# Causal attention of a two-layer kernel: scores from stacked split products, keys masked on GpSimd, values projected behind the experts

## Chip, cores and metric

One core of one Trainium2 chip. The metric is the device time of one execution in microseconds; the engines are TensorE (PE, its weight loads PEld), VectorE (DVE), ScalarE (ACT), GpSimd (POOL) and SyncE (SP, which here issues DMAs).

## The reference, cut to what matters

Two layers run on 16 sequences of 100 rows of 256 values. Each layer is a cross attention over a context and a mixture of experts, each on normed rows and added to them. The change touches the second layer's attention and its neighbours:

```python
qp = q @ Wq.T                                   # q: layernorm of x, 16 x 100 x 256
kv = latent_kv @ Wkv_expand.T                   # latents 64 wide -> keys and values of 256
...                                             # 16 heads of 16 columns
scores = einsum('bhqd,bhkd->bhqk', qh, kh) * HD ** -0.5
scores = where(tril(ones((100, 100))), scores, finfo.min)
out = einsum('bhqk,bhkd->bhqd', softmax(scores), vh)
...
return out @ Wout.T
```

Only the first 100 context rows of a sequence take part, since the mask is causal. Ahead of it stands the first layer's mixture of experts: 8 experts, two per row, hidden width 688.

## The kernel before

**Order of the stages.** After the first layer's attention comes the dispatch of the rows to experts (`Dispatch`, lines 1050 to 1391), in one block of `gated_moe`. Scores choose two experts for each row; products on TensorE (`tensor_lists`, line 1228) list which row goes to which place; DVE turns that into indices (lines 1378 to 1380), and POOL gathers the first 128 rows by an indirect DMA (line 1459). TensorE and ScalarE also make the keys (`project_keys`, 2106, moved by 2122) and values (`project_values`, 2115, moved by 2128) of the second layer's attention in that block, nine sequences' values ahead of the list products and seven behind. Each block ends with a barrier of all engines.

Then `gated_experts` takes up to 32 tiles of 128 rows. ScalarE and DVE split an expert's weights into a high and a low fp32r part (1682, 1729), TensorE multiplies three split products (`split_products`, 183), turns and multiplies down. ScalarE may begin a tile's weights when SP has announced that expert's load (`announce`, 1438); in the block SP issues two tiles' down weights (1444) and the loads of experts 5 to 7 (1433) first. The results come back by DMA and DVE adds them to X (1768).

**Norm and query projection.** `causal_attention` calls `layernorm`: on DVE a chain of small dependent instructions on 100x16 values (124 to 139, with a square root on ScalarE), the normed rows (143), transposes on TensorE, and the split into XH (ScalarE, 160) and XL (DVE, 149). In the next block DVE splits the query weights (2179, 2180), TensorE makes eight 128x400 pieces of the queries, six fp32r products each, and ScalarE and DVE copy four each to QT (2173, 2186).

**The attention loop.** 18 steps, pipelined over sequences i; each sequence has two halves u of 8 heads (n = 2i + u), and each half two groups g of 4 heads with a PSUM bank each.
- DVE `operands`: `kb` is the half's keys repeated for 8 heads, times 0 or 1 so that each head keeps its own 16 rows (2343, 128x800), and `qb` a copy of the queries (2345).
- PE `scores`: per group one fp32 product of 128 rows by 400 columns (2246) and one bf16 product that adds the causal mask (2248).
- DVE `maxima`: two reductions (2353) and a multiplication by -SCALE (2357).
- ACT `exps`: eight exponentials of 100x100 with their sums (2313).
- PE `turn`: eight transposes (2259); ACT and DVE `move` one bank each (2319, 2361); PE `values`: eight products of 16 columns (2272).
- DVE scales O (2389, 2394); PE turns it (2285), ACT copies it (2331), PE multiplies by Wout (2296), DVE adds X (2383).

The order on each engine is written out by hand in `step`. On PE it is scores(i, 0), transposes of O of i-2, turn and values of older halves, scores(i, 1), turn(2i), Wout, values.

Of the kernel before, what the change touches and what calls it, by code (L numbers as in the profile page):

```python
# [82 lines left out]

def layernorm(core, tag, X, XN, ident, XH, XL, known=0, loads=None, first=None, arrive=None, ident_in=None):

# [5 lines left out]
    with ExitStack() as ctx:  # L91
# [1371 lines left out]
def gated_moe(core, dram, X, ident, normed, results, causal):  # L1463

    nc = core.nc
    KEYS_FIRST, VALUES_FIRST = 5, 9
    with ExitStack() as ctx:
        weights = GatedWeights(core, ctx, dram)
        rows = GatedRows(core, ctx)
        with ExitStack() as stage:  # L1470
            d = Dispatch(core, ctx, stage, dram, "m0_", X, ident, E0, TOK0, False, normed,
                         (weights.rows, None, weights.places))
            latents = CausalLatents(core, stage, dram)
            with nc.Block() as block:

                @block.sync
                def _(sp):
# [8 lines left out]
                    weights.load_down(sp, d.tile_expert, 0)  # L1486
                    sp.wait_ge(d.rows_stored, 16)
# [9 lines left out]
                def _(pe):  # L1497
# [4 lines left out]
                    causal.project_values(pe, latents, range(VALUES_FIRST))  # L1502
                    d.tensor_lists(pe)
                    causal.project_values(pe, latents, range(VALUES_FIRST, B))

                @block.scalar
                def _(act):
# [4 lines left out]
                    causal.move_values(act)  # L1512
# [5 lines left out]
        gated_experts(core, X, ident, d, weights, rows, results, causal)  # L1518


def gated_experts(core, X, ident, d, weights, rows, results, causal):
# [9 lines left out]
    with ExitStack() as ctx:  # L1531
# [42 lines left out]
        with nc.Block() as block:  # L1574

            @block.sync
            def _(sp):
# [4 lines left out]
                for e in range(E0):  # L1582
                    weights.announce(sp, e)
# [28 lines left out]
            def _(pe):  # L1612
# [53 lines left out]
                down(k, 1)  # L1666

            @block.scalar
            def _(act):
# [48 lines left out]
                hidden_out(tiles - 1, 1)  # L1718

# [411 lines left out]

def causal_attention(core, dram, X, ident, causal, later):

    nc, psum = core.nc, core.psum
    HT = H // KD
    SCALE = HD ** -0.5
    wq, wo, mask, blocks, KTT, V = causal.wq, causal.wo, causal.mask, causal.blocks, causal.KTT, causal.V
    with ExitStack() as ctx:
        XH = fixed(ctx, nc, "XH_c", [P, KD, B * S], F32R)
        XL = fixed(ctx, nc, "XL_c", [P, KD, B * S], F32R)  # L2140
        wqh = fixed(ctx, nc, "c_wqh", [P, KD, D], F32R)
        wql = fixed(ctx, nc, "c_wql", [P, KD, D], F32R)
        maskb = fixed(ctx, nc, "c_maskb", [S, S], BF16)
        identb = fixed(ctx, nc, "c_identb", [S, S], BF16)
        QT = fixed(ctx, nc, "c_QT", [P, KD, B * S])

        with ExitStack() as stage:
            XN = fixed(stage, nc, "XN_c", [S, B, D])
            layernorm(core, "ln2_", X, XN, ident, XH, XL, B - 1, later)

        parts = core.sem("ca_parts")
        chain = core.sem("ca_chain")
        proj = core.sem("ca_proj")

        tiles = [(k, c) for c in range(NC) for k in range(KD)]

        with nc.Block() as block:

            @block.tensor
            def _(pe):  # L2160
                pe.wait_ge(parts, 1)
                for n, (k, c) in enumerate(tiles):
                    cols = slice(c * CH, (c + 1) * CH)
                    last = split_products(nc, psum[n][:, 0:CH], [(wqh[:, j, k * P:(k + 1) * P], wql[:, j, k * P:(k + 1) * P],
                                                                  XH[:, j, cols], XL[:, j, cols]) for j in range(KD)])
                    last.then_inc(proj, 1)

            @block.scalar
            def _(act):
                for n in range(0, len(tiles), 2):  # L2170
                    k, c = tiles[n]
                    act.wait_ge(proj, n + 1)
                    nc.scalar.activation(QT[:, k, c * CH:(c + 1) * CH], psum[n][:, 0:CH], ACT.Copy)

            @block.vector
            def _(v):
# [58 lines left out]
        with nc.Block() as block:  # L2235

            @block.tensor
            def _(pe):
# [99 lines left out]
            def _(v):  # L2338
# [28 lines left out]
                def step(i, w):  # L2367
                    n = i * 2
                    if has(i, 0, B - 1):
                        maxima(i, 0)  # L2370
# [193 lines left out]
```

## Time and profile before

| | us |
|---|---|
| median of 3 runs | 1821.97 (1820.47 to 1822.61) |
| profiled execution | 1817.92 |
| its span | 1816.1 |

| engine | busy share of the span |
|---|---|
| PE | 89% |
| PEld | 61% |
| DVE | 68% |
| ACT | 41% |
| POOL | 51% |

The span runs from the first to the last instruction of the profiled execution; the execution's own time is 1.8 us longer. Shares are averages over stages with different limits, so the rows below are read stage by stage: stretches of the span first, then groups of instructions of one stage, then single instructions in order of time. Times in the rows count from the span's start. A group's line gives its total and mean duration, and behind the second bar the idle time of its engine just before it with what ended that idle time.

### The profile page before, as it was taken

How to read it: one execution, taken by the hardware profiler on the slowest of the kernel's cores; microseconds unless marked ns; L12 is line 12 of the kernel's file. 1: busy time of each engine (PE TensorE's matmuls, PEld its weight loads, DVE VectorE, ACT ScalarE, POOL GpSimd, SP SyncE). 2: the span in 40 equal slices, each digit the busy share in tenths (PEclk: the TensorE clock that was granted, in tenths of full speed). 3: DMA queues.
4: the chain of work that ended last, by engine and by line, in shares of the span. 5: the costliest groups of instructions: out<-in, count | busy, mean ns of one | idle time of the engine just before them, and what ended most of it. 6: DMA issues, size and time to landing. Idle time of an engine off the chain costs nothing. (4 is left out here: it accounts for less than half of the span.)

```text
span 1816.1 us, 27644 instructions
## 1 busy us (share of the span) xinstructions
PE 1622.1 (89%) x8770; PEld 1110.5 (61%) x8770; DVE 1230.1 (68%) x2197; ACT 742.8 (41%) x1965; POOL 921.1 (51%) x799
## 2 busy tenths in 40 slices
PE   5999977999999999999999996799999289978980
PEld 4667744555555555555555553499999167665870
DVE  5598768777787777777787744466666757756433
ACT  3100102444444444444444452466666156652220
POOL 0377747777888777777888452023332000000636
PEclk9999987999999999999999997699999699988895
DMA  6434344122212221222212002664444420001443
GB/s 199 134 67 96 69 106 136 42 79 79 79 41 75 79 70 52 79 78 79 79 39 77 10 11 87 211 196 130 132 139 116 156 58 1 0 4 37 123 112 108
DMA packets 91472, 157.41 MB, mean 87 GB/s; under 512 B 45841, under 2 KB 70645, under 8 KB 88077
## 3 DMA queue, kind: packets, MB, share of 16 engines
q1 hardware_dynamic: 84301, 138.86, 26.2%
q0 software_dynamic: 7040, 16.92, 3.2%
q8 instruction: 67, 1.10, 0.3%
q14 instruction: 64, 0.52, 0.1%
HBM read 125.31 MB, written 28.48 MB: 85 GB/s over the span
## 5 line engine op out<-in xcount | busy, mean ns | idle before, releaser
L897 ACT ACTIVATE R<-banks 128x400 f32<-128x400 f32 x768 | 326.7, 509 | 317.9 <-PE banks L931 317.1
L713 DVE TENSOR_REDUCE PM<-banks 128x2 f32<-128x964 f32 x320 | 360.9, 1133 | 137.7 <-PE banks L690 137.6
L751 POOL TENSOR_TENSOR EA<-EA,R 128x400 f32<-128x400 f32 x288 | 306.1, 1063 | 119.2 <-ACT R L897 105.8
L931 PE MATMUL banks<-QS,KH 128*128 128x400 f32 x768 | 288.8, 376 | 2.3 <-DMA QB<-ML 2.3
L931 PE MATMUL banks<-QB,KB 128*128 128x400 f32 x768 | 265.7, 346 | 0.0
L731 DVE TENSOR_TENSOR banks<-banks,R 128x400 f32<-128x400 f32 x320 | 183.8, 574 | 27.9 <-ACT R L897 26.7
L540 POOL TENSOR_TENSOR arena<-arena 96x400 f32<-96x400 f32 x128 | 141.4, 1125 | 115.8 <-DVE arena L515 115.6
L941 PE MATMUL banks<-R,KV 128*64 128x400 f32 x960 | 187.5, 512 | 0.0
L931 PEld LDWEIGHTS banks<-QS,KH 128*128 128x128 f32 x768 | 145.1, 189 | 54.5 <-issue 38.0
L690 PE MATMUL banks<-KH,QS 64*128 64x482 f32 x320 | 160.6, 503 | 17.2 <-DVE PM L713 7.7
L690 PEld LDWEIGHTS banks<-KH,QS 64*128 64x128 f32 x320 | 60.7, 190 | 160.7 <-DVE PM L713 86.4
L690 PE MATMUL banks<-KH,QB 64*128 64x482 f32 x304 | 152.5, 502 | 0.0
L515 DVE TENSOR_TENSOR arena<-banks,rope_q 96x400 f32<-96x400 f32 x256 | 128.5, 561 | 33.4 <-PE banks L183 33.3
L931 PEld LDWEIGHTS banks<-QB,KB 128*128 128x128 f32 x768 | 145.7, 190 | 0.4
L1729 DVE TENSOR_TENSOR e_UL<-m_up,e_UH 128x696 fp32r<-128x696 f32 x128 | 107.0, 877 | 22.7 <-ACT e_UH L1682 22.7
L1598 POOL DMA_INDIRECT results<-e_ys,m_target x32 | 43.2, 1351 | 155.6 <-DVE e_ys L1742 155.6
L1157 POOL IOTA m_steps<- 100x13 f32 x2 | 0.3, 155 | 234.3 <-POOLq L71 234.3
L941 PE MATMUL banks<-R,arena 128*64 128x400 f32 x576 | 112.4, 512 | 0.0
L389 POOL TENSOR_TENSOR arena<-arena 128x722 f32<-128x722 f32 x60 | 103.6, 1729 | 17.3 <-DMA arena<-in_ctx_k 17.3
L941 PEld LDWEIGHTS banks<-R,KV 128*64 128x64 f32 x960 | 58.3, 136 | 74.8 <-ACT R L897 43.4
L2313 ACT ACTIVATE c_PR<-banks,c_nmax 100x100 f32<-100x100 f32 x256 | 84.1, 355 | 48.2 <-DVE c_nmax L2357 48.2
L183 PE MATMUL banks<-e_UH,e_xh 128*128 128x348 f32 x256 | 88.3, 345 | 8.2 <-DVE e_xl L1724 7.3
(288 smaller groups left out, 3239.0 us busy)
## 6 DMA issues: line engine op xcount, KB each, us to landing
arena<-in_ctx_T SPq DMA_DIRECT2D x16, 1444.0 KB
m_stage_d<-in_m_down SPq DMA_DIRECT2D x32, 672.0 KB
QS<-queries SPq DMA_DIRECT2D x16, 800.0 KB, 6.9
m_up<-in_m_up SPq DMA_DIRECT2D x8, 1392.0 KB, 13.0
queries<-q_out_h SPq DMA_DIRECT2D x64, 100.0 KB, 2.4
queries<-q_out_l SPq DMA_DIRECT2D x64, 100.0 KB, 2.4
QB<-queries SPq DMA_DIRECT2D x16, 400.0 KB, 8.7
arena<-recips SPq DMA_DIRECT2D x32, 200.0 KB
```

Source lines behind the costliest of these rows:

```text
L183: ins = nc.tensor.matmul(out, lhs, rhs, start=first and n == 0, stop=last and n == len(todo) - 1)
L389: ins = ops.tensor_tensor(raw[:, row, half], raw[:, row, half], ropeT[:, row, half], ALU.mult)
L515: last = nc.vector.tensor_tensor(prod[:, h % 2, n, :].rearrange("p (b s) -> p b s", b=CB), psum[2 * (h % 2) + half][0:HALF, 0:CH].rearrang ...
L540: last = nc.gpsimd.tensor_tensor(rot[:, h % TURNS, half, :], prod[:, h % 2, 2 * half, :], prod[:, h % 2, 2 * half + 1, :], ALU.add)
L690: last = nc.tensor.matmul(psum[f_bank(b, i) + f % 2][:, 0:KW], high[r][rows, t * P:(t + 1) * P], KH[r][rows, KAT[j]:KAT[j] + KW], start=Tr ...
L713: nc.vector.tensor_reduce(PM[:, 2 * i:2 * i + n], banks[:, k:k + n, 0:KW], AX.X, ALU.max).then_inc(red_done, 1)
L731: ins = nc.vector.tensor_tensor(acc, acc, tile_of(n, 0), ALU.add)
L751: nc.gpsimd.tensor_tensor(out, first, tile_of(n, 1), ALU.add).then_inc(odd_sum, 1)
L897: nc.scalar.activation(tile_of(n, o), psum[ring_bank(score_tile(b, n, o))][:, 0:CH], ACT.Exp).then_inc(exp_done, 1)
L931: last = nc.tensor.matmul(out, lhs[r][:, keys], heads[:, o], start=lhs is KH, stop=lhs is KB)
L941: last = nc.tensor.matmul(psum[CTX][o * DC:(o + 1) * DC, 0:CH], KV[b_mod(b)][:, t, :], tile_of(n, o), start=t == 0, stop=t == KT - 1)
L1729: nc.vector.tensor_tensor(split_part(UL, i), whole_part(e, i), as_f32(split_part(UH, i)), ALU.subtract).then_inc(ul_ready, 1)
```

## The change

1. Keys and queries are split into high and low fp32r parts. `SplitKeys` keeps, for each group of four heads, the high keys in the group's 64 partitions and the low keys in the other 64; the queries' high part is placed in both. So one fp32r product of 128 rows gives high by high and high by low, a second one of 64 rows adds low queries by high keys, and the mask product stays: six one-pass products per half.
2. The scale -SCALE goes into the query weights, the mask is turned in sign, and DVE takes minima, which are the exponentials' bias as they are; each group has its own semaphore count.
3. The key masking is on POOL (128x800 as before). DVE makes five query copies per half, four of them 64x100 between partition halves.
4. scores(i + 1, 0) stands half a step earlier on PE, behind turn(2i); turn(2i - 1), scores(i, 1) and values open the step. DVE's order follows.
5. The split of the keys: POOL in the norm's block (`first_keys`) and in the projection's, ScalarE and DVE in the projection's.
6. Values are projected at the end of the experts' block; the first five experts are announced at the end of the dispatch's block.

```diff
 def layernorm(...)
+            if pool_work:
+                @block.gpsimd
+                def _(pool):
+                    pool_work(pool)
...
 def gated_moe(...)
                     weights.load_down(sp, d.tile_expert, 0)
+                    for e in range(weights.EARLY):
+                        weights.announce(sp, e)
                     sp.wait_ge(d.rows_stored, 16)
...
                     causal.project_keys(pe, latents, range(KEYS_FIRST, NC * KD))
-                    causal.project_values(pe, latents, range(VALUES_FIRST))
                     d.tensor_lists(pe)
-                    causal.project_values(pe, latents, range(VALUES_FIRST, B))
...
-                    causal.move_values(act)
...
 def gated_experts(...)
-                for e in range(E0):
+                for e in range(weights.EARLY, E0):
                     weights.announce(sp, e)
...
                 down(k, 1)
+                pe.wait_ge(ht_ready, tiles * PARTS)
+                pe.wait_ge(y_done, tiles)
+                causal.project_values(pe, latents, range(B))
...
                 hidden_out(tiles - 1, 1)
+                causal.move_values(act)
...
+class SplitKeys:
+    def place_high(self, copy, done, c):
+        cols = slice(c * CH, (c + 1) * CH)
+        for k in range(KD):
+            for g in range(2):
+                rows = self.rows(g)
+                copy(self.KS[rows, k, g, cols], self.KTT[rows, k, cols]).then_inc(done, 1)
+    def leave_low(self, pool, c):
+        cols = slice(c * CH, (c + 1) * CH)
+        for k in range(KD):
+            for g in range(2):
+                rows = self.rows(g)
+                self.nc.gpsimd.tensor_tensor(self.KTT[rows, k, cols], self.KTT[rows, k, cols],
+                                             as_f32(self.KS[rows, k, g, cols]), ALU.subtract).then_inc(self.low, 1)
+    def place_low(self, eng, copy, c):
+        cols = slice(c * CH, (c + 1) * CH)
+        eng.wait_ge(self.low, (c + 1) * KD * 2)
+        for k in range(KD):
+            for g in range(2):
+                copy(self.KS[self.rows(1 - g), k, g, cols], self.KTT[self.rows(g), k, cols])
...
 def causal_attention(...)
+        def first_keys(pool):
+            split.place_high(nc.gpsimd.tensor_copy, split.high_pool, 0)
+            pool.wait_ge(split.high_pool, KD * 2)
+            split.leave_low(pool, 0)
+            split.place_high(nc.gpsimd.tensor_copy, split.high_pool, 1)
...
+                @block.gpsimd
+                def _(pool):
+                    pool.wait_ge(split.high_pool, 2 * KD * 2)
+                    split.leave_low(pool, 1)
+                    for c in (2, 3):
+                        pool.wait_ge(split.high_act, (c - 1) * KD * 2)
+                        split.leave_low(pool, c)
                 @block.scalar
                 def _(act):
+                    for c in (2, 3):
+                        split.place_high(copy_act, split.high_act, c)
+                    split.place_low(act, copy_act, 0)
+                    for n, (k, c) in enumerate(tiles):
+                        act.wait_ge(proj, n + 1)
+                        nc.scalar.activation(QH[:, k, c * CH:(c + 1) * CH], psum[n][:, 0:CH], ACT.Copy).then_inc(q_high, 1)
                 @block.vector
                 def _(v):
...
+                    for n, (k, c) in enumerate(tiles):
+                        cols = slice(c * CH, (c + 1) * CH)
+                        v.wait_ge(q_high, n + 1)
+                        nc.vector.tensor_tensor(QL[:, k, cols], psum[n][:, 0:CH], as_f32(QH[:, k, cols]), ALU.subtract)
+                        if k == KD - 1 and c:
+                            split.place_low(v, nc.vector.tensor_copy, c)
...
                 def scores(i, u):
-                        nc.tensor.matmul(out, qb[u][:], kb[u][:, g * HB:(g + 1) * HB, :].rearrange("p h s -> p (h s)"),
+                        nc.tensor.matmul(out, qd[u][:, g, :], kb[u][:, g].rearrange("p h s -> p (h s)"),
                                          start=True, stop=False)
+                        nc.tensor.matmul(out, ql[u][rows, :], kb[u][rows, g].rearrange("p h s -> p (h s)"),
+                                         start=False, stop=False)
...
                 def step(i, w):
+                    if has(i, 1, B):
+                        turn(n - 1, 1, False)
                     if has(i, 0, B - 1):
-                        scores(i, 0)
+                        scores(i, 1)
+                    if has(i, 1, B):
+                        values(i, n - 2, 0)
...
-                    if has(i, 1, B):
-                        turn(n - 1, 1, False)
-                        values(i, n - 2, 0)
                     if has(i, 0, B - 1):
-                        scores(i, 1)
                         turn(n, 0, isinstance(i, int) and i == 0)
+                    if has(i, 0, B - 2):
+                        scores(i + 1, 0)
...
+            @block.gpsimd
+            def _(pool):
+                def keys(i, u):
+                    if has(i, 1, B):
+                        pool.wait_ge(s_ready, n * 2 - 2)
+                    nc.gpsimd.tensor_tensor(kb[u][:], as_f32(KS[:, u, :, bass.ts(i, S)]).rearrange("p g (o s) -> p g o s", o=1)
+                                            .to_broadcast([P, 2, HB, S]),
+                                            heads[:].rearrange("p (g h o) -> p g h o", g=1, o=1)
+                                            .to_broadcast([P, 2, HB, S]), ALU.mult).then_inc(k_ready, 1)
...
+                def queries(i, u):
+                    if has(i, 1, B):
+                        v.wait_ge(s_ready, n * 2 - 2)
+                    at = bass.ts(i, S)
+                    for g in range(2):
+                        for half in range(2):
+                            nc.vector.tensor_copy(qd[u][split.rows(half), g, :], QH[split.rows(g), u, at])
+                    nc.vector.tensor_copy(ql[u][:], QL[:, u, at]).then_inc(q_ready, 1)
+                def minima(i, u):
+                    for g in range(2):
+                        v.wait_ge(s_ready, n * 2 + (g + 1))
+                        nc.vector.tensor_reduce(least[u][:, g * HB:(g + 1) * HB],
+                                                bank_heads(psum[SC + 2 * u + g][0:S, 0:HB * S]), AX.X,
+                                                ALU.min).then_inc(min_ready, 1)
-                    nc.vector.tensor_scalar(nmax[u][:, 1, :], nmax[u][:, 0, :], -SCALE, None, ALU.mult).then_inc(neg_ready, 1)
```

## Rows read from the trace of the kernel before

**Rows 1.** Stretches by stage: busy us of PE, PEld, DVE, ACT, POOL; clock; DMA

```profile
1413.00:1440.00 27.00, 0.00 (x0) 0.00 (x0) 19.66 (x49) 0.09 (x1) 0.97 (x1) 0.54 0.39 127
...
1452.50:1466.30 13.80, 11.46 (x48) 11.08 (x48) 3.66 (x8) 2.09 (x5) 0.00 (x0) 0.75 0.73 145
1484.00:1620.00 136.00, 124.40 (x944) 95.67 (x942) 94.35 (x221) 92.15 (x497) 0.00 (x0) 1.00 0.00 0
```

**Rows 2.** Groups of the attention stretch: busy, mean ns | idle before, releaser

```profile
L2313 ACT ACTIVATE c_PR<-banks,c_nmax 100x100 f32<-100x100 f32 x256 | 84.1, 355 | 48.2 <-DVE c_nmax L2357 48.2
...
L2343 DVE TENSOR_TENSOR c_kb<-c_KT,c_blocks 128x800 f32<-128x800 f32 x32 | 31.7, 991 | 1.2 <-PEq L2157 0.4
...
L2345 DVE COPY c_qb<-c_QT 128x100 f32 (+1 forms) x32 | 6.6, 205 | 0.0
...
L2357 DVE TENSOR_SCALAR c_nmax<-c_nmax 100x8 f32<-100x8 f32 x32 | 5.5, 172 | 1.1
```

**Rows 3.** Tile c_PR: ns min/median/max, first and last start

```profile
L2313 ACT ACTIVATE c_PR<-banks,c_nmax x256: 333/352/425, 1470.8 to 1617.2; 100x100 f32<-100x100 f32 x128
```

**Rows 4.** Timeline of one attention step: start us, us, engine, line

```profile
1530.93 0.90 PE L2246 MATMUL banks<-c_kb,c_qb 128*100 128x400 f32 x2
...
1532.68 0.33 PE L2285 MATMUL banks<-ident,c_O 100*128 100x100 f32 x2
...
1534.41 0.34 ACT L2313 ACTIVATE c_PR<-banks,c_nmax 100x100 f32<-100x100 f32 x1 [2.56 <-DVE c_nmax L2357]
...
1536.99 0.54 ACT L2319 ACTIVATE c_PT<-banks 100x400 f32<-100x400 f32 x1
...
1537.62 0.86 PE L2259 MATMUL banks<-ident,c_PR 100*100 100x100 f32 x8 [0.82 <-ACT c_PR L2313]
...
1540.55 0.90 PE L2246 MATMUL banks<-c_kb,c_qb 128*100 128x400 f32 x2
```

**Rows 5.** Timelines, end of the dispatch and start of the experts

```profile
1161.31 0.19 DVE L1378 CAST m_foundu<-banks 128x32 uint32<-128x32 f32 x1 [2.31 <-PE banks L1228]
...
1162.69 1.15 POOL L1459 DMA_INDIRECT e_xg<-normed,m_source  x1 [40.08 <-DVE m_target L1380]
...
1152.66 0.38 ACT L2128 ACTIVATE c_V<-banks 100x256 f32<-100x256 f32 x1 [1.26 <-PE banks L2115]
...
1167.53 0.38 ACT L2128 ACTIVATE c_V<-banks 100x256 f32<-100x256 f32 x1 [0.47 <-PE banks L2115]
1173.22 1.46 ACT L1682 ACTIVATE e_UH<-m_up 128x696 fp32r x2 [5.30 <-SPq L1438]
```

**Rows 6.** Stretch between the list products and the barrier, columns as in rows 1

```profile
1157.00:1163.00 6.00, 6.00 (x74) 4.21 (x73) 2.98 (x7) 1.85 (x5) 0.31 (x1) 0.50 0.00 0
```

**Rows 7.** Groups on POOL by shape: busy, mean ns | idle before

```profile
L751 POOL TENSOR_TENSOR EA<-EA,R 128x400 f32<-128x400 f32 x288 | 306.1, 1063 | 119.2 <-ACT R L897 105.8
...
L782 POOL TENSOR_TENSOR arena<-arena 128x800 f32<-128x800 f32 x15 | 28.4, 1896 | 0.0
```

**Rows 8.** Timelines of L408 without and with POOL beside it

```profile
291.11 0.91 DVE L408 TENSOR_TENSOR KB<-arena,KH 64x722 fp32r<-64x722 f32 x1 [0.49 <-ACT KH L414]
...
337.04 2.72 POOL L751 TENSOR_TENSOR EA<-EA,R 128x400 f32<-128x400 f32 x2 [1.03 <-ACT R L897]
...
337.43 1.42 DVE L408 TENSOR_TENSOR KB<-arena,KH 64x722 fp32r<-64x722 f32 x1
```

**Rows 9.** Timeline of the norm's chain and the query projection's end

```profile
1440.40 0.19 DVE L124 TENSOR_TENSOR ln_small<-stats 100x16 f32<-100x16 f32 x1
...
1443.28 5.26 DVE L143 TENSOR_SCALAR XN_c<-X,ln_small 100x256 f32<-100x256 f32 x16
...
1461.16 0.35 PE L183 MATMUL banks<-XH_c,c_wql 128*128 128x400 f32 x1
...
1465.01 0.34 PE L183 MATMUL banks<-XH_c,c_wql 128*128 128x400 f32 x1
1465.39 0.57 DVE L2186 COPY c_QT<-banks 128x400 f32<-128x400 f32 x1 [1.62 <-PE banks L183]
```

More of the change, by code:

```diff
@@ L1516, in _, with gated_experts @@
                     d.vector(v)
-        gated_experts(core, X, ident, d, weights, rows, results, causal)
-def gated_experts(core, X, ident, d, weights, rows, results, causal):
+        gated_experts(core, X, ident, d, weights, rows, results, causal, latents)
+def gated_experts(core, X, ident, d, weights, rows, results, causal, latents):
     nc, psum = core.nc, core.psum
@@ L2157, in causal_attention @@
[L2157 to L2176, printed above, removed]
-                do = Chain(v, chain)
-                v.wait_ge(causal.loaded, 16 * 4)
-                do(nc.vector.tensor_copy(wqh[:], wq[:]))
-                nc.vector.tensor_tensor(wql[:], wq[:], as_f32(wqh[:]), ALU.subtract).then_inc(parts, 1)
-                nc.vector.tensor_copy(maskb[:], mask[:])
-                nc.vector.tensor_copy(identb[:], ident[0:S, 0:S])
-                for n in range(1, len(tiles), 2):
-                    k, c = tiles[n]
-                    v.wait_ge(proj, n + 1)
-                    nc.vector.tensor_copy(QT[:, k, c * CH:(c + 1) * CH], psum[n][:, 0:CH])
@@ L2189, in causal_attention, with copy_act @@
-        qb = [fixed(ctx, nc, f"c_qb{u}", [P, S]) for u in range(2)]
-        kb = [fixed(ctx, nc, f"c_kb{u}", [P, HT, S]) for u in range(2)]
-        nmax = [fixed(ctx, nc, f"c_nmax{u}", [S, 2, HT]) for u in range(2)]
+        heads = fixed(ctx, nc, "c_heads", [P, HB])
+        split = SplitKeys(core, ctx, causal)
+        KS = split.KS
+        QH = fixed(ctx, nc, "c_QH", [P, KD, B * S], F32R)
+        QL = fixed(ctx, nc, "c_QL", [P, KD, B * S], F32R)
+        def copy_act(out, src):
+            return nc.scalar.activation(out, src, ACT.Copy)
@@ L2363, in _ @@
                 v.sem_inc(x_done, 1)
[L2364 to L2365 removed]
+                queries(0, 0)
+                queries(0, 1)
+                minima(0, 0)
+                queries(1, 0)
                 def step(i, w):
                     n = i * 2
[L2369 to L2372 removed]
                     if has(i, 1, B):
@@ L2375, in step @@
                     if has(i, 0, B - 1):
-                        maxima(i, 1)
+                        minima(i, 1)
                     if has(i, 0, B - 2):
-                        operands(i + 1, 1)
-                    if has(i, 0, B - 1):
-                        move(n, 0)
-                    if has(i, 2, B + 1):
-                        v.wait_ge(y_ready, i)
-                        nc.vector.tensor_tensor(X[:, i - 2, :], psum[LB][0:S, 0:D], X[:, i - 2, :], ALU.add).then_inc(x_done, 1)
+                        queries(i + 1, 1)
                     if has(i, 1, B):
```

125 lines of the change are left out of this document (84 added, 41 removed).

## Prediction

> **What bounds the kernel now.** I first cut the trace into stages, in a table of stretches. The change touches four: the dispatch ahead of the experts, the 27 us after the experts' last product, norm and query projection, and the causal attention. In the attention stretch TensorE is busy 124.4 of 136 us at clock 1.00, DVE 94.4, ScalarE 92.2, POOL nothing [rows 1]. Then the groups of that stretch: ScalarE's exponentials idle 48.2 us, put down to the sign change of the maxima [rows 2]. That is a symptom. The timeline of one step shows the loop: scores at 1530.93, the first score product of the next step at 1540.55, so 9.62 us a step, in which TensorE stands still 0.82 us, before a transposition that waits for ScalarE [rows 4]. The rest is TensorE work in its own order: scores (u=0), transposes, values, scores (u=1), transposes, output product, values. ScalarE waits because the next scores stand behind values on TensorE. So the loop is TensorE's, plus one stall.
>
> **Scores.** One half's scores last from 1530.93 to 1532.68, 1.75 us [rows 4]: two fp32 products and two mask products. Afterwards there are six one-pass products of 400 columns (four fp32r, two bf16). In the query projection 21 gaps between fp32r products of that width take 1465.01 - 1461.16 = 3.85 us, 0.18 each [rows 9]. Six are 1.08 us, so 0.67 saved per half, 1.34 per step. The scores of u=0 are also made half a step ahead, so the exponentials no longer follow the values, and the 0.82 us stall goes. TensorE's step becomes 9.62 - 0.82 - 1.34 = 7.46, call it 7.4.
>
> Would another engine be later? ScalarE: eight exponentials run from 1534.41 to 1536.99, 2.58 us, a move lasts 0.54 [rows 4]; twice both and the copy of O transposed, about 0.5, make 6.7 us. It gets a new order to bear: its second eight stand behind that copy, whose transposes TensorE now makes after scores and values; 0.7 us of slack is left, so no stall. DVE: 94.35 us in 136 [rows 1], 6.7 a step. The change takes away key masking (31.7 us), query copies (6.6) and sign changes (5.5) [rows 2], over 16 steps 2.7 each: down to 4.0. It adds ten query copies a step. A copy of 100 columns lasts 0.205 us [rows 2]; overlapped it might cost 0.12, held apart 0.205, so 1.2 to 2.1 us a step. I take the upper one, the row's own duration: 6.1, under 7.4. POOL: two masks a step of 128x800; the same form takes 1.90 us there [rows 7]; 3.8 us under 7.4.
>
> **The unseen wait.** No row has a POOL multiplication beside a DVE copy between SBUF tiles. The nearest is the key addition of L408, also DVE reading SBUF: 0.91 us alone, 1.42 us beside POOL, while two POOL additions there took 2.72 instead of 2.1 us [rows 7, 8]. One waits for the other to end. The mask of a half starts as its scores end; the copies come 0.7 us later, after the minima, and could wait up to 1.4 us, or not at all. I take that they wait: it is what the nearest row shows. Two such waits would make 6.1 + 2.8, above 7.4; but a DVE that comes later meets less of the mask, and its results are needed a half later, so it settles near 1 us behind and TensorE still sets 7.4. The Trainium skill ("SBUF — State Buffer", "Who interferes with whom") has a copy in a two-port mode and a GpSimd instruction fully block each other, whoever comes second; by that the waits are there and the sum is as given, and without it the first rival's. It speaks against this change.
>
> First to last exponential is now 146.4 us [rows 3], 2.3 of them within the last eight. 15.5 steps at 7.4 and 2.3 make 117. **Loop: -29.** The first steps give some back: the first scores need a POOL mask (1.9 us [rows 7], not DVE's 1.0 [rows 2]), and the first ten copies interlock with two masks: **+3** (0 to 6). TensorE will have stood about 10 us before them instead of 2, so it starts at 1.2 GHz, as the projection did behind the norm (mean clock 0.75 there, 1.00 in the loop, [rows 1]): **+2**.
>
> **Dispatch.** Sixteen value products and their copies leave it. The copies end at 1167.91 and are its last work; the row gather ends at 1163.84 [rows 5]. The list products also come earlier: half of them need only DVE's first comparison of two, but values stood before them, and DVE waited 2.31 us for them; half, 1.15, goes. The gather then ends at 1162.7, 5.2 us before the old end. The announcing of the first five experts moves before the barrier: now ScalarE waits 5.30 us for it, behind seven DMA issues on SP. Their loads have landed by then: the queues move nothing from 1157 to 1163 [rows 6], so SP waits for nothing that lasts. 5.2 + 5.3 = 10.5, less about 1 for the barrier's passing and the first gathered rows: **-9.3**. If the barrier stayed, -5.3; at best -10.5. Later loads and gathers keep their order on SP and POOL.
>
> **Values moved: 0.** The copies ran from 1152.66 to 1167.91, at half clock [rows 5, 6]. After the experts TensorE is idle, and ScalarE all but idle, for 27 us while DVE adds the results [rows 1]. Were that cover gone, up to 15.
>
> **Norm: +5.** POOL now makes eight copies and four subtractions of 64x400 in this block. No POOL copy is in the trace; the 400-column addition takes 1.06 us [rows 7]; I take 0.6 for a copy (one input) and 1.06 as upper end, 9 to 13 us in all, about the 12 from 1440.40 [rows 9] to the projection at 1452.50 [rows 1]. But the norm's small chain runs beside it: twelve dependent instructions from 1440.40 to 1443.28 [rows 9], eight with two SBUF inputs, the kind of [rows 8]. Each of the eight meets a running POOL instruction and waits 0.5 to 1 us: 4 to 8, less where POOL passes during the square root. I take 5; at no waiting 0, at worst 9.
>
> **Projection: +5.5.** Today it ends with a copy of 0.57 us at 1465.39 [rows 9]. Afterwards ScalarE places 12 pieces first, which cold TensorE covers. DVE gets eight subtractions instead of four copies, and twelve copies of 64x400 (0.36 us: 0.15 fixed and half of 0.42 for 400 columns, an estimate from the copy in [rows 2] and PSUM copies of 0.57). The last four, behind the last subtraction, add 1.5 us, and DVE falls behind by 1 to 2 in all; meeting twelve POOL subtractions of 1.06, the weights' split adds 1 and the first placed copies up to four times 1.06. Ends +1.5 and +8.
>
> **Sum.** -29 + 3 + 2 - 9.3 + 0 + 5 + 5.5 = -22.8. The profiled execution took 1817.92 us (span 1816.1), 4.05 below the median of the runs; against the median of 1821.97 it makes 1799.
>
> **Rivals.**
> *The copies and small instructions hardly wait.* POOL and DVE share less than the one row suggests, which has two SBUF inputs. Then the first steps cost 0, norm 2, projection 2: 1822 - 29 + 2 - 9.3 + 4 = 1790.
> *POOL is slower than its row.* The mask reads both operands repeated over a dimension; the row's operands are plain. At 2.5 us DVE's waits grow past what the lag absorbs, a step takes 7.9 and the first steps 6 more, with norm and projection 3 longer: 1799 + 7.8 + 6 + 3 = 1815.
> *The products aren't one-pass.* If the stacked products took as long as the fp32 ones, TensorE's step is 8.7, only the stall and part of the order gained: +1.3 x 15.5 = 20 more, 1819. The projection's spacing speaks against.
> *Slower: masks and copies lock each other in a row.* If a mask takes over about 3.4 us, the copies no longer fit between two masks; scores, mask, copies and scores follow each other, and the step is two masks and two copy groups, at 3.8 us 2 x (3.8 + 1) + some 1.9 for the scores between, 11.5: (11.5 - 7.4) x 15.5 = 64 more, 1863. It decides from 9.0 us a step on: the loop then gains 6, as much as the other terms cost together. The 1.90 us row speaks against; no row has such operands on POOL.
>
> **Chances.** Forecast 0.48, no waits 0.25, slower POOL 0.14, no one-pass gain 0.05, interlock 0.08. The likeliest time is 1799. The range takes the terms' ends and the first two rivals: 1781 to 1817, leaving the last two out. Under 0.2% (3.6 us; the three runs lie 2.1 apart) a measurement can't tell: faster 0.87, same 0.05, slower 0.08.
>
> **What would show it.** Score products spaced 0.18 us and a step near 7.4; TensorE's idle time gone from the transposes; masks of 1.9 us on POOL with DVE's first query copy of a half ending with the mask. ScalarE's first weight split about 0.5 us after a barrier near 1163. The norm's small chain longer than 2.9 us, each instruction ending just after a POOL instruction. Wrong if the mask lasts over 2.5 us, if the copies run beside it at 0.2 us, or if the step stays above 8.

## The result, and the profile after

The changed kernel takes 1893.91 us, median of 4 runs (1881.92 to 1899.53), against 1822.11 for the kernel before: ratio 1.038, 95% interval 1.036 to 1.040. It is 72 us slower; forecast were 23 us faster. The profiled execution took 1881.92 us (span 1880.1), 64 us more than the profiled execution before. The other three executions, 1890.69 to 1899.53, have no profile, so what follows accounts for the 64 us.

The stretches that answer to [rows 1], behind the experts, the projection and the loop, then slices of the loop (columns as in [rows 1]):

```profile
1408.00:1435.50 27.50, 7.25 (x33) 5.14 (x32) 19.61 (x48) 6.13 (x16) 0.97 (x1) 0.70 0.38 124
1452.50:1472.20 19.70, 11.07 (x48) 10.69 (x48) 15.68 (x25) 10.33 (x20) 12.88 (x12) 0.77 0.52 104
1490.00:1660.00 170.00, 170.00 (x821) 129.35 (x822) 106.15 (x248) 83.37 (x443) 38.04 (x26) 0.58 0.00 0
...
1520.00:1530.00 10.00, 10.00 (x55) 7.88 (x55) 6.59 (x17) 6.16 (x34) 2.72 (x2) 0.60 0.01 2
1530.00:1540.00 10.00, 10.00 (x75) 7.40 (x73) 9.12 (x24) 6.84 (x36) 3.04 (x2) 1.00 0.00 0
1540.00:1550.00 10.00, 10.00 (x51) 7.70 (x51) 7.30 (x18) 6.16 (x34) 3.04 (x2) 0.59 0.00 0
1550.00:1560.00 10.00, 10.00 (x47) 7.80 (x46) 5.20 (x12) 2.58 (x14) 1.52 (x1) 0.50 0.00 0
```

In the loop TensorE is busy in 170 of 170 us, so by the profile no other engine holds it up (a product whose weight load comes late is recorded from that load on, as shown below, so such a wait counts as busy). But its mean granted clock is 0.58, where the loop before had 1.00. In finer slices it is 0.50 (1.2 GHz) from 1470 to 1528, 1.00 (2.4 GHz) to about 1542, 0.50 to 1579, 1.00 to 1593, 0.50 to 1661, 1.00 to 1675. It rises and falls while TensorE goes through the same steps without a pause. The tile of the exponentials says what that costs; the row answers to [rows 3]:

```profile
L2399 ACT ACTIVATE c_PR<-banks,c_least x256: 333/347/449, 1478.5 to 1677.9; 100x100 f32<-100x100 f32 x128
```

199.4 us from first to last instead of 146.4. Where the 64 us lie, counted from block to block: the dispatch's block starts 2.4 us later (before any work of the change), ScalarE's first weight split comes 7.55 us sooner after that start, the experts take 0.8 longer, the norm's block 4.2, the projection's 6.2, the first exponential comes 1.7 later after the loop's block begins, the loop takes 53 more from first to last exponential, and what stands behind the last exponential 3.3 more; that makes the 64.

Then one half's scores at clock 1.00, which answer to the first lines of [rows 4] (timeline; PE lines are products, PEld lines their weight loads):

```profile
1530.09 0.17 PEld L2327 LDWEIGHTS banks<-c_kb,c_qd 128*100 128x100 f32 x1
1530.12 0.40 PE L2327 MATMUL banks<-c_kb,c_qd 128*100 128x400 f32 x1
1530.45 0.16 PEld L2329 LDWEIGHTS banks<-c_kb,c_ql 64*100 64x100 f32 x1 [0.19 <-issue]
1530.45 0.42 PE L2329 MATMUL banks<-c_kb,c_ql 64*100 64x400 f32 x1
1530.80 0.12 PEld L2331 LDWEIGHTS banks<-c_maskb,c_identb 100*100 100x100 bf16 x1 [0.20 <-issue]
1530.81 0.37 PE L2331 MATMUL banks<-c_maskb,c_identb 100*100 100x400 bf16 x1
1530.85 0.17 PEld L2327 LDWEIGHTS banks<-c_kb,c_qd 128*100 128x100 f32 x1
1530.87 0.49 PE L2327 MATMUL banks<-c_kb,c_qd 128*100 128x400 f32 x1
...
1531.86 0.53 PE L2354 MATMUL banks<-c_V,c_PT 100*100 x5
```

The six products last from 1530.12 to 1531.86, 1.74 us: as long as the fp32 products before (1.75), not 1.08. The 64-row product's load begins only with its own product, 0.33 us after the product before it, and the next load (mask, 1530.80) again. The load behind a mask product does not wait. So even at full clock a step is 8.53 us (1530.12 to 1538.65). At clock 0.50 the same half lasts 2.93 us:

```profile
1551.81 0.64 PE L2327 MATMUL banks<-c_kb,c_qd 128*100 128x400 f32 x1
...
1554.74 1.07 PE L2354 MATMUL banks<-c_V,c_PT 100*100 x6
```

and a step 15.6 us. 15.5 steps at 8.53 and 2.3 make 134.5 us; measured are 199.4. So there are two losses: products that are no shorter, and the clock, which costs 65 us.

### The profile page after: what moved, and what is told of

Read it like the earlier page. It is cut to its first block and busy times, and to the rows that moved or that the text cites. A ratio compares the mean times of both kernels' runs of the same rounds, so it can differ in the third digit from the quotient of the medians.

```text
span 1880.1 us, 27960 instructions
## 1 busy us (share of the span) xinstructions
PE 1686.9 (90%) x8770; PEld 1159.2 (62%) x8770; DVE 1273.5 (68%) x2278; ACT 753.0 (40%) x1981; POOL 990.5 (53%) x855
## 5 line engine op out<-in xcount | busy, mean ns | idle before, releaser
L2429 POOL TENSOR_TENSOR c_kb<-c_KS,c_heads 128x800 fp32r<-128x800 f32 x32 | 48.6, 1519 | 152.1 <-PE banks L2331 146.0
L1690 ACT ACTIVATE e_UH<-m_up 128x696 fp32r x128 | 92.8, 776 | 13.5 <-PEq L1480 13.3
L189 PE MATMUL banks<-XH_a,AH 128*96 128x400 f32 x256 | 91.1, 356 | 3.0 <-DVEq L506 3.0
```

The source lines that it names most:

```text
L1690: nc.scalar.activation(split_part(UH, i), whole_part(e, i), ACT.Copy).then_inc(w_hi, 1)
```

## The experiments

Two theories on the products (the spacing comes from the 64 rows, or from the operands), and three on the clock: the work of the loop brings it down; TensorE enters cold and doesn't recover; DVE and POOL lock each other and hold TensorE.

**128 rows everywhere (r1).**

```diff
-nc.tensor.matmul(out, ql[u][rows, :], kb[u][rows, g]...
+nc.tensor.matmul(out, ql[u][:], kb[u][:, g]...
```

> The low product of each group is made over all 128 rows instead of the group's 64; it then also adds the other group's low queries times this group's low keys, which the changed kernel leaves out. Rows theory: even at granted clock 1.00 the changed kernel's six products of a half take 1.74 us (starts 1530.12 to 1531.86), because the weight load of each 64-row product, and of the product behind it, begins only when the product before it has ended (loads at 1530.45 and 1530.80, each with its own product). With 128 rows everywhere the loads lie beside the products: spacing 0.17 to 0.18, a half near 1.1 us, and a step in stretches at clock 1.00 about 8.5 - 1.2 = 7.3 us; at 0.50 a step of 15.6 falls to about 14. If the clock divides as in the changed kernel (some 4 steps in 10 at full clock) the time falls by about 25 us, to some 1865. Rival (the spacing comes from the operands, fp32r queries as weights or keys as moving data, not from the rows): spacing stays at 0.33 and the time within 5 us of the changed kernel's at like clock.

1803.15 us (1795.46 to 1807.2), ratio to before 0.988, 0.985 to 0.991: 91 us faster than the changed kernel by one line. Timeline of a half:

```profile
1545.13 0.40 PE L2327 MATMUL banks<-c_kb,c_qd 128*100 128x400 f32 x1
1545.19 0.17 PEld L2329 LDWEIGHTS banks<-c_kb,c_ql 128*100 128x100 f32 x1
1545.37 0.34 PE L2329 MATMUL banks<-c_kb,c_ql 128*100 128x400 f32 x1
1545.38 0.12 PEld L2331 LDWEIGHTS banks<-c_maskb,c_identb 100*100 100x100 bf16 x1
1545.55 0.33 PE L2331 MATMUL banks<-c_maskb,c_identb 100*100 100x400 bf16 x1
...
1546.26 0.35 PE L2354 MATMUL banks<-c_V,c_PT 100*100 x3
```

and the stretch behind the clock's rise:

```profile
1510.00:1600.00 90.00, 90.00 (x818) 83.76 (x818) 86.21 (x239) 76.93 (x424) 35.00 (x23) 1.00 0.00 0
```

Every load now lies beside the product ahead of it; the spacing is 0.18, the half 1.13 us, the step 7.32 (1530.49 to 1537.81). The rows theory holds. And the clock, 0.50 in most of 1472 to 1505, then stays at 1.00 to the loop's end, which the expectation had not counted on: it gave 1865.

**Longer products again (r2).**

```diff
-nc.tensor.matmul(out, qd[u][:, g, :], kb[u][:, g]...
+nc.tensor.matmul(out, as_f32(qd[u][:, g, :]), as_f32(kb[u][:, g]...
```

> The first score product of each group is read as fp32 instead of fp32r, everything else as in the changed kernel, so TensorE gets back the longer products of the kernel before at the same place. Work theory (the loop is at 1.2 GHz because of what TensorE does there since its long fp32 products are gone): granted clock 1.00 through the loop, a step of 8.5 + 4 x 0.5 = 10.5 us, first to last exponential about 165 instead of 199 us, time near 1848: faster with more work. Entry theory (TensorE stands 9.8 us before its first scores and stays low from then): clock as low as in the changed kernel, each of four products a step about 1 us longer at 1.2 GHz, first to last exponential over 230 us, time above 1920. Lock theory (query copies held by the GpSimd masks): clock low, time at or above 1882.

1840.98 us, ratio 1.010 (1.008 to 1.011): 53 us faster than the changed kernel with more work on the engine that bounds it. The stretch:

```profile
1490.00:1640.00 150.00, 150.00 (x1000) 101.38 (x1000) 118.25 (x282) 93.14 (x506) 42.55 (x28) 1.00 0.00 0
```

Clock 1.00, step 10.49 us, first to last exponential 164.4, all as the work theory had it (the time is 7 us below its 1848), though this loop also entered at 0.50 and keeps the four 64-row products of a step.

**The pause ahead of the loop filled**, first with narrow products that start once DVE has made its first low queries (r3):

```diff
+pe.wait_ge(q_low, 1)
+for _ in range(40): nc.tensor.matmul(psum[0][:, CH:512], wqh[:, 0, 0:P], XH[:, 0, 0:512 - CH], ...)
...
+for _ in range(14): nc.tensor.matmul(psum[SC][0:S, 0:HB * S], identb[:], maskb...)
 scores(0, 0)
```

> TensorE's pause ahead of the loop is filled: 40 products of 112 columns behind the query projection's last one and 14 mask products ahead of the first scores, whose results are overwritten or not read. Nothing else changes. Entry theory: the loop begins at clock 1.00 and stays there, a step of 8.53 us as in the changed kernel's stretches at full clock, first to last exponential about 135 us, time near 1818. Work theory: the loop begins at 1.00 and falls to 0.50 within the first few steps although TensorE never stands still; mean clock of the loop about 0.6 as in the changed kernel, time within 15 us of 1885.

1893.9 us, ratio 1.036 (1.032 to 1.040), no change from the changed kernel. But the clock fell to 0.50 at 1472, behind a pause of 1.7 us at the block's barrier, ahead of the first scores (1474.25): the loop didn't begin warm, so this tests nothing of the entry. So a wider filling, first on the kernel of r1 (r5):

```diff
-for _ in range(40): nc.tensor.matmul(psum[0][:, CH:512], wqh[:, 0, 0:P], XH[:, 0, 0:512 - CH], ...)
+for _ in range(30): nc.tensor.matmul(psum[0][:, 0:CH], wqh[:, 0, 0:P], XH[:, 0, 0:CH], ...)
...
-for _ in range(14): nc.tensor.matmul(psum[SC][0:S, 0:HB * S], identb[:], maskb...)
+for _ in range(18): nc.tensor.matmul(psum[SC][0:S, 0:HB * S], identb[:], maskb...)
```

> The low product over 128 rows, as in the run before with 1803 us, and TensorE's pause ahead of the loop filled with work of full width: 30 fp32r products of 400 columns behind the query projection's last, 18 mask products ahead of the first scores; their results are overwritten. In the run without the filling the loop began at clock 0.50 and had it in most of its first 30 us (1472 to 1504), then 1.00 to the end. Work theory: the loop keeps 1.00 by itself once its steps are short, so that only the beginning is left to gain: first to last exponential about 120 instead of 125 us, or a little under that, time 1788 to 1798. If the pause at the barrier (1.7 us in the other filled run) is enough to bring the clock down again: 1800 to 1805, no change.

1795.27 us (1794.21 to 1795.78), ratio 0.986 (0.984 to 0.987). The pause at the barrier is 0.81 us here, not 1.70, so the width and the pause changed together. The clock is 1.00 up to 1480, dips to a mean of 0.66 in 1480 to 1490, where the first steps wait, and is 1.00 from then on; first to last exponential 118.2 us. The loop behind the dip:

```profile
1490.00:1590.00 100.00, 100.00 (x907) 92.95 (x907) 96.04 (x266) 85.12 (x471) 38.58 (x26) 1.00 0.00 0
```

This is the fastest version of the study and beats both kernels. The same filling on the changed kernel, with its own 64-row products (r10):

> The changed kernel's own scores, with the full-width filling that kept the clock at 1.00 ahead of the loop in the run with 1795 us (30 fp32r products of 400 columns, 18 mask products). The earlier filled run, with 112 columns, reached the loop at 0.50 and so didn't test its theory. Entry theory: loop begins at 1.00 and stays, step 8.53, first to last exponential about 135 us, time near 1815. Work theory: begins at 1.00, falls to 0.50 within a few steps and then goes up and down as in the changed kernel; first to last exponential 180 to 205 us, time 1870 to 1895.

1878.18 us (1877.02 to 1881.72), ratio 1.031 (1.030 to 1.033). Stretches:

```profile
1470.00:1475.00 5.00, 4.02 (x22) 2.60 (x22) 4.50 (x11) 1.28 (x1) 3.00 (x2) 1.00 0.00 2
1475.00:1480.00 5.00, 3.67 (x19) 1.85 (x18) 4.46 (x9) 2.72 (x16) 3.04 (x2) 1.00 0.00 0
1480.00:1490.00 10.00, 8.57 (x34) 5.64 (x35) 7.83 (x21) 8.77 (x50) 3.04 (x2) 0.56 0.01 2
...
1530.00:1540.00 10.00, 10.00 (x82) 8.08 (x82) 9.59 (x23) 6.46 (x36) 4.30 (x3) 0.97 0.00 0
1540.00:1550.00 10.00, 10.00 (x44) 7.53 (x42) 5.99 (x17) 6.37 (x35) 1.52 (x1) 0.50 0.00 0
```

It begins at 1.00, falls within the first steps, and goes up and down as in the changed kernel (199.5 us from first to last exponential). The fall in the first steps r5 has too; but r5 is back at 1.00 after about 7 us and stays there, while this loop comes back after about 44 us and falls again after about 14. By the medians the filling is worth 8 us (r1 to r5) to 16 us (changed kernel to r10), not the rest. Of the 16 the profiles show nothing: the two profiled executions (1881.92 and 1881.72 us) and their loops (199.4 and 199.5) are alike.

**Masks on DVE (r4).**

```diff
 def queries(i, u):   # DVE
+    nc.vector.tensor_tensor(kb[u][:], KS..., heads..., ALU.mult).then_inc(k_ready, 1)
-def keys(i, u):      # GpSimd
```

> The key masks are made on DVE, ahead of the query copies of the same half; GpSimd does nothing in the loop. Lock theory: no copy waits any more (0.2 us each instead of up to 1.48), TensorE isn't held at the loop's start, clock 1.00, DVE about 8 us a step, step 8.5 to 9, time 1818 to 1830. Work theory: copies at 0.2 us, yet the clock of the loop stays mostly at 0.50 and TensorE stays busy all the time; time within 15 us of the changed kernel's, 1880 to 1905. First scores come 0.5 to 2 us earlier in both.

1888.26 us, ratio 1.035 (1.033 to 1.037). The copies no longer wait:

```profile
L2436 DVE CAST c_qd<-c_QH x128: 197/207/211, 1470.5 to 1674.1; 64x100 fp32r x96, 64x100 fp32r<-64x100 f32 x32
```

211 ns at most, where the changed kernel has up to 1475. The first scores start at 1471.8 instead of 1476.1 and the first exponential at 1474.1 instead of 1478.5, more than the 0.5 to 2 us expected. Yet the clock is as low and the time within the changed kernel's own runs: the lock is real, takes part in the loop's late start, and costs the steps nothing (15.6 us at 0.50 and 8.5 at 1.00 in both kernels). What it costs steps as short as r1's isn't tested: there DVE is busy in 86 of 90 us, waits inside its instructions included.

**Other order of the six products** (128, 128, 64, 64, mask, mask; r7):

```diff
 # the order in words
-for g in range(2): qd product, ql product, mask product
+for g in range(2): qd product
+for g in range(2): ql product
+for g in range(2): mask product
```

> The changed kernel with the six products of a half in another order: both 128-row products, both 64-row products, both mask products. At granted clock 1.00: if a weight load is exposed only where the height changes (64 rows after 128, and back), two loads of about 0.17 us are exposed instead of four and a half lasts about 1.4 us (1.74 before, 1.13 with 128 rows everywhere); if every 64-row product and its successor pay, three are, about 1.55 us; if the order does nothing, 1.74. A step at 1.00 is then 7.8 to 8.2 instead of 8.53 us. Time, by how long the clock is high, between 1815 and 1880; if the clock falls as often as in the changed kernel, near 1870.

1819.19 us, ratio 0.997 (0.994 to 1.000): 75 us faster than the changed kernel with the same six products. The ten runs lie between 1798.24 and 1824.53, presumably by when the clock rose: the shortest has a mean granted clock of 0.934 over its span, the longest 0.921, but only one was profiled. At 1.00 (timeline):

```profile
1545.59 0.59 PE L2326 MATMUL banks<-c_kb,c_qd 128*100 128x400 f32 x2
1546.10 0.43 PE L2330 MATMUL banks<-c_kb,c_ql 64*100 64x400 f32 x2
1546.46 0.54 PE L2333 MATMUL banks<-c_maskb,c_identb 100*100 100x400 bf16 x2
...
1546.84 0.35 PE L2356 MATMUL banks<-c_V,c_PT 100*100 x3
```

A half lasts 1.25 us, less than any of the three expectations. The two 64-row products together last 0.43 us, where one alone lasted 0.42: one has the first 64 partitions, the other the second 64, and they run side by side. In the profiled execution the clock rose at 1521 and stayed. With r5's filling as well (r11):

> The grouped order (128, 128, 64, 64, mask, mask) with the same full-width filling ahead of the loop. The scores are the changed kernel's, nothing left out or added. Without the filling a half lasted 1.25 us at clock 1.00 and the clock, once risen, stayed; its runs lay between 1798 and 1824 us, by when it rose. If it holds from the start: a step of 7.5 us, first to last exponential about 120 us, time 1796 to 1801 with a small spread. If the loop falls back at its beginning, where the first steps wait for the masks: 1808 to 1822, spread as before.

1807.75 us (1804.2 to 1810.52), ratio 0.993 (0.9915 to 0.994): the second case, 0.25 us below its range. The clock began at 1.00, was 0.60 in 1480 to 1490 and 0.50 in 1490 to 1500, and stayed at 1.00 from about 1502 to the end.

**No 64-row products at all (r8).**

```diff
-nc.tensor.matmul(out, ql[u][rows, :], kb[u][rows, g]..., start=False, stop=False)
```

> The changed kernel without the low products (low queries by high keys are left out of the scores; DVE still makes the low copies). Every score product then has 100 or 128 rows, and TensorE has less work a step than in any kernel so far. Rows theory (the 64-row products with their exposed loads bring the clock down and stretch the step): clock 1.00 for most of the loop, four products at 0.17 to 0.18, a half 0.75 us, TensorE's step 6.6 us but DVE full at about 7.2, time 1795 to 1803. Rival (the clock falls when the score products are too few): clock mostly 0.50 as in the changed kernel, first to last exponential over 160 us, time above 1840.

1799.57 us, ratio 0.988 (0.987 to 0.990); clock 1.00 from 1506 to the loop's end, step 6.66 (1540.11 to 1546.77), DVE busy 77.6 of 80 us. TensorE has less work a step than in the changed kernel and keeps its clock, so "too few score products" is not the reason.

**64 rows for 16 columns only (r9).**

```diff
-nc.tensor.matmul(out, ql[u][rows, :], kb[u][rows, g]...)
+nc.tensor.matmul(out[:, 0:16], ql[u][rows, :], kb[u][rows, g]...[:, 0:16])
+nc.tensor.matmul(out[:, 16:], ql[u][:], kb[u][:, g]...[:, 16:])
```

> The changed kernel's low product is cut in two: 16 columns over the group's 64 rows, the other 384 over all 128 rows (these also add the other group's low queries times this group's low keys). So two changes of height per group remain, as in the changed kernel, but hardly any column goes through 64 rows. Waiting theory (what brings the clock down is that the array stands while weights load at each change of height): four loads stay exposed, a half about 1.13 + 4 x 0.17 = 1.8 to 1.9 us at clock 1.00, a step 8.7 to 8.9, and the clock falls back to 0.50 as in the changed kernel; time above 1865. Height theory (400 columns over half the rows bring it down): the same step of 8.7 to 8.9 us, but clock 1.00 once risen; first to last exponential 145 to 155 us, time 1825 to 1840. If the small products' loads are not exposed: step 7.5, time 1803 to 1808.

Seven runs from 1826.99 to 1882.41: three at 1827, in the height theory's range, two at 1844, two at 1880 and 1882, in the waiting theory's; the five shorter have a ratio of 1.008 (1.004 to 1.011). The profiled one is the longest. Its clock was 0.50 until 1638 and 1.00 from there to the loop's end, with the expected step of 8.71 us. When the clock rises decides the time, and one profile doesn't tell the theories apart. So the same with r5's filling (r13):

> As r9 (16 low columns through 64 rows, 384 through 128, four exposed loads a half, a step of 8.71 us at clock 1.00, against 8.53 in the changed kernel), with the full-width filling of r10 ahead of the loop. Height theory: the loop begins at 1.00, may dip in its first steps where TensorE waits for masks, and then holds 1.00 to its end; first to last exponential 135 to 145 us, time 1818 to 1830, executions close together. Waiting theory: as in r10 it falls within the first steps and goes up and down, first to last exponential 180 us or more, time 1865 to 1885.

1851.66 us (1843.29 to 1860.27), ratio 1.017 (1.013 to 1.022), 164.7 us from first to last exponential: neither theory's numbers. Stretches:

```profile
1500.00:1510.00 10.00, 10.00 (x42) 8.09 (x42) 5.67 (x12) 5.47 (x31) 2.69 (x2) 0.50 0.01 2
1510.00:1520.00 10.00, 10.00 (x83) 8.44 (x83) 8.68 (x21) 5.31 (x30) 3.37 (x3) 0.97 0.00 1
...
1570.00:1580.00 10.00, 10.00 (x78) 8.31 (x78) 9.22 (x23) 7.64 (x44) 3.60 (x3) 1.00 0.00 0
1580.00:1590.00 10.00, 10.00 (x69) 8.07 (x68) 7.91 (x20) 7.64 (x43) 2.65 (x3) 0.78 0.00 0
1590.00:1600.00 10.00, 10.00 (x49) 8.41 (x47) 6.17 (x13) 2.13 (x11) 2.88 (x2) 0.50 0.00 0
```

It held 1.00 for some 75 us, then fell without a pause. So a loop with exposed loads and hardly any 64-row columns can fall back too, later than the changed kernel does (about 14 us each time). That the 400 columns through 64 rows count as well would fit this, but one profile doesn't show it.

**The parts around the loop.** The dispatch part alone, on the kernel before (r6):

```diff
 # in words
 kernel before
+the diff's parts in gated_moe and gated_experts (values behind the experts, early announcing)
```

> The kernel before with only the dispatch part of the change: values projected behind the experts, the first five experts announced in the dispatch's block, the latents kept; norm, projection and attention as before. In the changed kernel's profile the first weight split stood 7.55 us earlier counted from the dispatch block's start, and that start itself 2.4 us later, the norm's block 4.35 us earlier. If the later start is chance (waits for DMAs ahead of the block), the part is worth 6.5 to 7.5 us: 1815 to 1817. If the start is later because of the change: 4 to 5 us, 1818 to 1819. If values behind the experts cost there: about 1822.

1814.32 us, ratio 0.9955 (0.994 to 0.997): 7.9 us gained by the medians, a little more than the 6.5 to 7.5 expected. So the later start of the dispatch in the changed kernel's profile is chance. The other profiles say the same: the block's first small instruction on DVE starts at 1122.2 us in the kernel before, at 1124.6 in the changed kernel, and anywhere from 1120.9 to 1124.1 in the thirteen runs, though no edit stands ahead of it.

The version of r5 with GpSimd's work out of the norm (r12):

```diff
-layernorm(..., pool_work=first_keys)
+layernorm(...)
 @block.gpsimd   # the projection's block
+first_keys(pool)
```

> The version with 1795 us (low product over 128 rows, filling ahead of the loop), with GpSimd's eight copies and four subtractions taken out of the norm's block and put at the head of its work in the projection's block. Lock theory (each DVE instruction on SBUF that meets a running GpSimd instruction ends with it): the norm's small chain goes back from 5.4 to 2.9 us, the sixteen normed rows from 6.9 to 5.3, so the projection's block begins about 3.5 to 4.2 us earlier; GpSimd then has 22 us instead of 13.7 there, DVE's placed copies wait for it, and that block lasts 5 to 8 us longer: 1796 to 1800, a little slower. Rival (the chain is long for another reason, the work in the norm costs nothing): chain stays 5.4, projection longer by 5 to 8, 1800 to 1804.

1802.55 us, ratio 0.989 (0.987 to 0.991). The norm's chain is back from 5.4 to 2.9 us, the block 4.2 shorter, the projection's block 6.6 longer. The chain decides for the lock theory, although the time lies above its 1796 to 1800 and in the rival's range. Not all of the 7 us to r5 (6 between the two profiles) belong to the move: the two blocks make 2.4 of them. TensorE's filling ended 8.9 us before the loop's block here, the clock was 0.50 again, and the first exponential came 2 us later after the block's start; another 2 us stand ahead of the norm, in the chance start of the dispatch. By the 2.4 us the norm is the cheaper place for this work.

## Why the prediction was wrong

**The step that failed: "Six are 1.08 us"**, and with it "TensorE's step becomes ... 7.4" (by the forecast's own sign it is wrong "if the step stays above 8"). The 0.18 us came from 128-row products [rows 9] and was applied to products of 64 rows, which no row showed. Measured: 1.74 us a half, a step of 8.53. With 128 rows it is 1.13 and 7.32: the price was right for the shape it was measured on. At full clock this costs 15.5 x 1.1 = 17 us. The Trainium skill ("TensorE: Matmul & The Clock Gate", "Part 3: Packing small matmuls — row/col tiling") says that products in different rows of the array run at once; in its list of what overlaps, a load runs beside a product only when the rows differ, while its paragraph on the mechanism also names a background buffer for weights. The pair that lasted 0.43 us agrees with the first; the 128-row loads, which do overlap 128-row products, speak against the list's "only".

**The second, larger miss: "it starts at 1.2 GHz, as the projection did"**, for 2 us, with full clock taken for granted behind it. The granted clock averaged 0.58 and that cost 65 us (134.5 to 199.4). The 17 and the 65, less the 2 allowed for a cold start, are the 80 us by which the loop missed its forecast. The rival "products aren't one-pass" (1819) had about the right step, 8.7, but assumed full clock too; no rival had the clock. What the runs show of it: the clock fell back in mid-loop only where weight loads are exposed four times a half and the products are one-pass (the changed kernel, r3, r4, r10, r13; in r9's profile, with such loads too, it rose late and held 1.00 for the 43 us that were left); past the first steps it never fell back where the rows were 128 throughout (r1, r5, r12), where the 64-row products stood side by side (r7, r11) or were gone (r8), nor beside longer fp32 products (r2). How the chip decides it, these runs don't settle.

**The unseen wait: right.** POOL's mask and DVE's copies lock each other:

```profile
1555.13 1.52 POOL L2429 TENSOR_TENSOR c_kb<-c_KS,c_heads 128x800 fp32r<-128x800 f32 x1 [6.94 <-PE banks L2331]
1555.47 1.23 DVE L2451 CAST c_qd<-c_QH 64x100 fp32r x1
```

The copy takes 1.23 us and ends with the mask, as the Trainium skill's "SBUF — State Buffer", "Who interferes with whom", has it. The mask is 1.52, not 1.90, so the interlock rival (from 3.4 us on) never came near; and in the steps DVE lags without holding TensorE.

**Norm: +5 forecast, 4.2 measured.** Timeline of the chain that answers to [rows 9]:

```profile
1435.57 2.24 POOL L2160 CAST c_KS<-c_KT 64x400 fp32r<-64x400 f32 x4 [25.73 <-POOLq L1579]
...
1436.28 0.42 DVE L131 TENSOR_SCALAR ln_small<-ln_small 100x16 f32<-100x16 f32 x1
...
1437.90 4.45 POOL L2167 TENSOR_TENSOR c_KT<-c_KT,c_KS 64x400 f32<-64x400 f32 x4
1438.09 0.89 DVE L136 TENSOR_SCALAR ln_small<-ln_small 100x16 f32<-100x16 f32 x1
...
1441.49 6.86 DVE L149 TENSOR_SCALAR XN_c<-X,ln_small 100x256 f32<-100x256 f32 x16
```

POOL's four subtractions last 1.11 each; the 0.17-us instruction of L136 takes 0.89 and ends with the first of them, 1438.98. The mechanism was right, its victims partly not, and that the sum came out near is partly luck. Six of the chain's twelve instructions were held, three of them with one SBUF tensor, which I had left out; five of the eight with two were not. So the chain lost 2.6 us, not 5; the other 1.6 are the normed rows, 6.86 us instead of 5.26 [rows 9], for which I had counted nothing.

**Projection: +5.5, measured 6.2. First steps: +3, measured 1.7. Values moved: 0, right**; their copies stand in the 27 us behind the experts and lengthen nothing.

**Dispatch: -9.3 forecast, -7.55 measured in the profile and -7.9 alone.** The announcing was gone from ScalarE's path:

```profile
1163.76 1.15 POOL L1465 DMA_INDIRECT e_xg<-normed,m_source  x1 [38.78 <-DVE m_target L1386]
...
1168.05 1.46 ACT L1690 ACTIVATE e_UH<-m_up 128x696 fp32r x2 [13.33 <-PEq L1480]
```

The gather came 1.3 us earlier after the block's start (1.15 forecast), but ScalarE starts 3.1 us after the gather's end at 1164.91, where I had allowed about 1 for the barrier and the rows. What fills it I didn't find.

Outside the loop, the forecast's -9.3 + 0 + 5 + 5.5 + 3 = +4.2 stands against -7.55 + 0.8 + 4.2 + 6.2 + 1.7 = +5.35. The loop with its cold start, -29 + 2, stands against +53; the other 2.4 and 3.3 of the 64 us lie ahead of these stages and behind them. With 128 rows the same change takes 1803, and 1795 with the pause ahead of the loop filled, on either side of the forecast of 1799; there the loop takes 118.2 us, against 117 in the forecast. One shape without a row, and the clock behind it, made the difference.

## What to carry to other kernels

Price a product by a row of the same number of rows, not of the same columns and type: a 64-row product between taller ones exposed its own weight load and the next here (a half of 1.74 us instead of 1.13). Put partial-height products next to one another on different rows (1.25 us), or give them the full height, and look at the granted clock ahead of the busy share: this TensorE was busy in 170 of 170 us at 0.58 of its speed. Where TensorE is the bound, carry a rival in which its clock falls, with the step's time at either level.

## What the runs showed that I had not expected

- One line of code, 64 rows or 128 for a product of 400 columns, moved the time by 91 us (1893.91 to 1803.15).
- More work made the kernel faster: fp32 instead of fp32r products, 1893.91 to 1840.98 us.
- TensorE's clock fell from 1.00 to 0.50 in a loop in which TensorE was busy in 10 of 10 us by the profile, and rose again in it, also without a pause.
- Two 64-row products of 400 columns on different halves of the partitions lasted 0.43 us together, 0.42 one alone.
